# Gate products moved among the last query sums, next key projection at the loop's end, mask begun beside the taps

## The reference, cut to what matters

```
q = silu(conv4(x @ Wq.T));  k = silu(conv4(x @ Wk.T));  v = silu(conv4(x @ Wv.T))
q = q * rsqrt(sum(q*q) + 1e-6);  k = k * rsqrt(sum(k*k) + 1e-6)      # per head
delta = delta_rule(q, k, v, beta)                                    # chunked, T = (I + tril(kb k'))^-1
paths = (fir3(v), fir63(v), delta, v)
gate_in = concat([x] + [mean and var per head of each path])         # 256 + 32 columns
hmid = gelu(gate_in @ gate_w1.T + gate_b1)                           # 512 wide
probs = softmax((hmid @ gate_w2.T + base_bias) / temp)               # 4 paths per head
x1 = layernorm(x + rmsnorm(sum(probs * paths)) @ Wo.T)
```

## Time and profile before

| | us |
|---|---|
| median of 3 runs | 1892.97 (1891.18 to 1901.68) |
| the profiled execution | 1894.72 |
| its span | 1893.0 |
| PE busy (matmul) | 1496.2 (79%) |
| DVE busy | 1315.3 (69%) |
| ACT busy | 950.1 (50%) |
| POOL busy | 440.7 (23%) |

### The profile page before, as it was taken

How to read it: one execution, slowest core, us unless ns; L and a number is a source line. 1 busy time by engine, 2 the same in 40 slices (tenths; PEclk the granted TensorE clock), 3 DMA queues, 4 the chain that set the end, 5 groups by cost and what they waited for, 6 DMA issues and landing times. The chain is left out here.

```text
span 1893.0 us, 40332 instructions
## 1 busy us (share of the span) xinstructions
PE 1496.2 (79%) x12507; PEld 1108.8 (59%) x12508; DVE 1315.3 (69%) x3331; ACT 950.1 (50%) x1998; POOL 440.7 (23%) x473
## 2 busy tenths in 40 slices
PE   6775165979999999999999999887436999999800
PEld 3445134747747747657557567476225888888700
DVE  6995155677787887887887887875455555554488
ACT  6772061356555644654655555542443555555434
POOL 6884200000030040040030210300223333333300
PEclk9997585989999999999999999998758999999955
DMA  5558642023243243333333333232524533333295
GB/s 197 190 163 256 154 101 58 3 67 94 71 127 92 62 122 102 78 91 101 87 89 106 95 106 90 79 97 76 196 91 140 192 105 101 104 104 101 77 385 190
DMA packets 297370, 224.34 MB, mean 119 GB/s; under 512 B 173472, under 2 KB 265632, under 8 KB 296960
## 3 DMA queue, kind: packets, MB, share of 16 engines
q1 hardware_dynamic: 225600, 158.84, 29.0%
q0 software_dynamic: 15232, 43.53, 6.4%
q10 hardware_dynamic: 56384, 19.93, 4.1%
HBM read 130.42 MB, written 91.82 MB: 117 GB/s over the span
## 5 line engine op out<-in xcount | busy, mean ns | idle before, releaser
L1462 DVE SCALAR_TENSOR_TENSOR B_conv<-B_ps_x,B_cw,B_conv 128x511 f32<-128x511 f32 (+2 forms) x192 | 143.5, 748 | 65.9 <-ACT B_conv L1176 59.3
L2031 POOL DMA_INDIRECT y_d<-C_yb,C_dest x136 | 132.1, 971 | 232.0 <-ACT C_yb L2142 229.7
L422 POOL DMA_INDIRECT xs_d<-x,slot_u x128 | 133.4, 1042 | 137.4 <-DVE m_acc L1857 100.6
L688 POOL MEMSET B_z<- 128x256 f32 (+4 forms) x40 | 5.5, 191 | 674.6 <-DMA B_z<-scr_a 674.6
L1176 ACT ACTIVATE B_conv<-B_ps_x,B_cw 128x512 f32<-128x512 f32 x64 | 43.7, 683 | 167.6 <-PE B_ps_x L745 167.3
L2261 DVE TENSOR_TENSOR C_av<-C_sg,C_ps_g 128x256 f32<-128x256 f32 x136 | 57.3, 421 | 94.6 <-ACT C_sg L2136 94.6
L2065 PE MATMUL C_ps_g<-C_w_high,C_xt_high 128*128 x272 | 119.5, 439 | 0.4 <-issue 0.4
L745 PE MATMUL B_ps_x<-B_xa,B_wk 128*128 128x512 f32 x128 | 67.5, 655 | 63.8 <-DVE B_sel L1454 44.9
L2273 DVE TENSOR_TENSOR C_avt_low<-C_ps_a,C_avt_high 128x256 fp32r<-128x256 f32 x136 | 57.7, 425 | 83.5 <-ACT C_avt_high L2131 83.5
L2065 PE MATMUL C_ps_g<-C_w_high,C_xt_low 128*128 x272 | 107.7, 396 | 0.0
L2065 PE MATMUL C_ps_g<-C_w_low,C_xt_high 128*128 x272 | 107.0, 393 | 0.0
(11 more groups left out here) (330 smaller groups left out, 4250.6 us busy)
## 6 DMA issues: line engine op xcount, KB each, us to landing
C_xb<-xs_d SPq DMA_DIRECT2D x136, 132.0 KB, 2.1
C_w_high<-y_d SPq DMA_DIRECT2D x12, 1024.0 KB, 14.1
A_band<-fir_long POOLq DMA_DIRECT2D x32, 256.0 KB, 5.9
A_work<-xT SPq DMA_DIRECT2D x16, 512.0 KB, 5.0
v_d<-A_v_tok SPq DMA_DIRECT2D x16, 512.0 KB, 3.5
short_d<-A_sh_tok SPq DMA_DIRECT2D x16, 512.0 KB, 3.2
B_xa<-xT SPq DMA_DIRECT2D x8, 1024.0 KB, 5.8
B_v_tok<-v_d SPq DMA_DIRECT2D x8, 1024.0 KB, 5.5
```

What stands on the lines that cost most here:

```text
L422: pool.indirect_dma_start(t["xs_d"][:, :], bass.IndirectOffsetOnAxis(ap=slot_u[:, c:c + 1], axis=0), x1[:, b, j, :], None).then_inc(done, 16)
L1462: V.scalar_tensor_tensor(conv[:, g % 2, k:], X[g % 2][:, :SEQ - k], cw[:, g // 4, gg % CH, 3 - k:4 - k], conv[:, g % 2, k:], ALU.mult, ALU ...
L2031: pool.indirect_dma_start(t["y_d"][:, :], bass.IndirectOffsetOnAxis(ap=dest[:, q:q + 1], axis=0), yb[:, u], None).then_inc(y_out[u], 16)
```

## The change

- **Gate on four banks.** The hidden chunks get four banks, `hidden = (X[0], X[1], B3, B4)`, and PE's gate splits into `from_x` (the two products with x of one chunk) and `from_stats` (the product with the statistics). The four `from_x` of the first half move out of the gate into `stage1b`, among the last query sums: one after the sum of group 5, three after that of group 6. The spins that stood there (two after each of the groups 5 to 7 and three after `rank`) go, and two take their place behind group 7. The last step, which prepares no pair, runs them inside its gate.
- **First key projection.** `project(i + 2, 0)` moves from the start of the next step to the end of this one, behind the second product; its wait for `x_out` goes. The spins at that place go from four to two, and the last two steps have none.
- **Mask.** It no longer waits for `mt_in[1]`; instead it waits for the count of `mixd` that DVE's first `weigh` gives.

```diff
+        hidden = (X[0], X[1], B3, B4)
...
                 def mask_at(p):
 
                     pool.wait_ge(at_kept, 8 * (p + 1))
-                    pool.wait_ge(mt_in[1], 32 * (p + 1))
+                    need(pool, mixd, 4 * (p - 1) + 1)
...
+                def from_x(i, b, c):
+                    pe.wait_ge(xg_in[b], 16 * (i + 1))
+                    for k in range(CH):
+                        mm(hidden[c][:], w1x[:, k, c * P:(c + 1) * P], xg[b][:, k, :], start=k == 0, stop=False)
+
+                def from_stats(c):
+                    mm(hidden[c][:], w1s[:, c * P:(c + 1) * P], st_t[:], start=False, stop=True).then_inc(gate_mm, 1)
...
-                    for g in range(5, 8):
-                        select(p, g)
-                        if last is not None:
-                            if g == 5:
-                                pe.wait_ge(a_kept[1], 4 * (p + 1))
-                            spin(B3, 2)
+                    if first:
+                        for g in range(5, 8):
+                            select(p, g)
+                    else:
+                        select(p, 5)
+                        for k in a_kept:
+                            pe.wait_ge(k, 4 * (p + 1))
+                        from_x(p - 1, 0, 2)
+                        select(p, 6)
+                        from_x(p - 1, 0, 3)
+                        pe.wait_ge(taps, 24 * p + 21)
+                        from_x(p - 1, 0, 0)
+                        pe.wait_ge(taps, 24 * (p + 1))
+                        from_x(p - 1, 0, 1)
+                        select(p, 7)
+                        spin(B5, 2)
                     turn_norms(p, 1)
                     if last is not None:
                         rank(last)
-                        spin(B3, 3)
...
+                def gate(i, has_prev, has_next):
+
+                    if has_prev:
+                        pe.wait_ge(rt, RT * (i - 1) + 1)
+                    pe.wait_ge(st_dve, ST * (i + 1))
+                    turn_stats(i, 0)
+                    if not has_next:
+                        pe.wait_ge(taps, 24 * (i + 1))
+                        for c in range(HID_CH):
+                            from_x(i, 0, c)
+                    pe.wait_ge(st_kept, 2 * i + 1)
+                    for c in range(HID_CH):
+                        from_stats(c)
+                    turn_stats(i, 1)
+                    for c in range(2):
+                        pe.wait_ge(gelu_ok, 8 * i + c + 1)
+                        from_x(i, 1, c)
...
+                    logits(i, 0)
+                    pe.wait_ge(st_kept, 2 * i + 2)
+                    for c in range(2):
+                        from_stats(c)
+                    for c in range(2, HID_CH):
+                        from_x(i, 1, c)
+                        from_stats(c)
+                    pe.wait_ge(raw_kept, 2 * i + 1)
+                    logits(i, 1)
...
-                    if has_next:
-                        hold(pe, x_out, 16 * (i + 1))
-                        project(i + 1, 0)
                     merges(i, has_prev, has_next)
...
                     if has_next:
                         at_rest(i + 1)
-                        spin(X[1], 4)
...
+                    if has_after:
+                        project(i + 2, 0)
+                        spin(X[1], 2)
```

More of the change, by code:

```diff
@@ L996, in recur, with turn_stats @@
                         within(i, s)
[L998 to L1002, removed]
+                def turn_stats(i, b):
                     for j in range(TPB):
@@ L1006, in gate, with logits @@
                     w.then_inc(st_turned, 1)
-                    pe.wait_ge(xg_in[b], 16 * (i + 1))
+                def logits(i, b):
+                    pe.wait_ge(gelu_ok, 8 * i + 4 * (b + 1))
                     for c in range(HID_CH):
[L1009 to L1022, removed]
+                        w = mm(B2[c * LANE:(c + 1) * LANE, :], w2[:, c, :], hid[:, c, :], start=True, stop=True)
+                    w.then_inc(raw_mm, 1)
+                def gate(i, has_prev, has_next):
[14 more added lines that the diff above has]
+                        from_x(i, 1, c)
+                    if has_next:
                         for k in a_kept:
@@ L1026, in gate @@
                         pe.wait_ge(r_ub, 4 * (i + 1))
-                    for c in range(HID_CH):
-                        w = mm(B2[c * LANE:(c + 1) * LANE, :], w2[:, c, :], hid[:, c, :], start=True, stop=True)
-                    w.then_inc(raw_mm, 1)
+                    logits(i, 0)
[7 more added lines that the diff above has]
+                    logits(i, 1)
                 def turn_logits(i, b, has_prev, has_next):
@@ L1112, in _, with step @@
                 select(0, 3)
-                stage1b(0)
+                stage1b(0, first=True)
                 at_first(0)
                 at_rest(0)
-                def step(i, has_prev, has_next):
-                    if has_next:
-                        hold(pe, x_out, 16 * (i + 1))
-                        project(i + 1, 0)
+                project(1, 0)
+                def step(i, has_prev, has_next, has_after):
                     merges(i, has_prev, has_next)
@@ L1133, in step @@
                         rank(i - 1)
-                    for b in range(2):
-                        gate(i, b, has_prev, has_next)
+                    gate(i, has_prev, has_next)
                     if has_next:
@@ L1311, in recur, with gate, keep_stats @@
                             keep_x1(i - 1, 1)
-                def gate(i, b):
-                    half = 2 * i + b
-                    act.wait_ge(st_turned, half + 1)
-                    need(act, gate_mm, 4 * half)
-                    A(st_t[:], TR[0:3 * STATS, :], ACT.Copy).then_inc(st_kept, 1)
-                    need(act, raw_mm, half)
-                    for c in range(HID_CH):
-                        act.wait_ge(gate_mm, 4 * half + c + 1)
-                        A(hid[:, c, :], X[c % 2][:], ACT.Gelu, bias=b1[:, c:c + 1]).then_inc(gelu_ok, 1)
-                    act.wait_ge(raw_mm, half + 1)
-                    A(raw_logits[:, b, :], B2[:], ACT.Copy).then_inc(raw_kept, 1)
+                def gate(i):
+                    def keep_stats(b):
+                        act.wait_ge(st_turned, 2 * i + b + 1)
+                        need(act, gate_mm, 8 * i + 4 * b)
+                        A(st_t[:], TR[0:3 * STATS, :], ACT.Copy).then_inc(st_kept, 1)
+                    keep_stats(0)
+                    for b in range(2):
+                        need(act, raw_mm, 2 * i + b)
+                        for c in range(HID_CH):
+                            act.wait_ge(gate_mm, 8 * i + 4 * b + c + 1)
+                            A(hid[:, c, :], hidden[c][:], ACT.Gelu, bias=b1[:, c:c + 1]).then_inc(gelu_ok, 1)
+                        if b == 0:
+                            keep_stats(1)
+                        act.wait_ge(raw_mm, 2 * i + b + 1)
+                        A(raw_logits[:, b, :], B2[:], ACT.Copy).then_inc(raw_kept, 1)
                 def rms(i, b):
@@ L1410, in step @@
                         keep_routes(i - 1)
-                    for b in range(2):
-                        gate(i, b)
+                    gate(i)
                     A(warm[:], eps5[:], ACT.Exp)
```

11 lines of the change are left out of this document (6 added, 5 removed).

## The result

| | before | after |
|---|---|---|
| median, us | 1893.07 (1891.18 to 1901.68) | 1932.24 (1929.17 to 1936.42) |
| profiled execution | 1894.72 | 1934.13 |
| span | 1893.0 | 1932.4 |
| ratio of the times | | 1.0199, 95% interval 1.0161 to 1.0237 |

Slower, as forecast, but by 39 us instead of 21, and outside the range (1880 to 1926).

What follows compares the result with a forecast made beforehand. What delays the norm on DVE was taken to delay everything, the gate being hidden but for 0.67 us. Six steps of +4 us gave 1919, 1917 as median, less 6 times 0.4: 1914 us; range 1880 to 1926.

Steps and rivals of the forecast that it cites:

- signs that it named for being right: Sums 5.7 us apart, norm waiting 3, no softmax or tap wait, PE idle 4 before merge at clock 0.5, slower merge.
- Term 1: Last query sums on PE: three x product pairs between the sums of groups 6 and 7 delay the norm by 3.2 us.
- Term 2: DVE's holes at logits, exponential and first tap pay back 0.67, 0.6 and 1.45 us; in sum the 3.2 us, no more.
- Term 3: PE before the merge: work ends at 832.8, loads land at 839.1, so PE idles about 6 us (3.5 to 7.5).
- Term 4: Merge on PE begins at the low clock: L897 4.8 us later, about 4 us lost a step (3 to 5.5).
- the first rival, a cured fall: The clock's fall before L936 goes away, a step gains 2.5 of its 4 us: 1902 us; chance 0.22.
- The start of the block … I count as zero: Start of the block, where the projection had warmed the clock: no change in time.
- The first pass: First of the loop's seven passes, without spins among the sums and with a later gate: zero (0 to +3 us).
- the cure of 2.4: Taken off the sum because some steps may lose their clock fall before L936: 6 times 0.4 us.
- The rival of the held clock: Clock stays at 1.00 through the merge, 0.5 to 3 us gained a step: 1871 to 1889 us; chance 0.23.

Runs made afterwards that it cites:

- e3: The changed kernel with the sum of group 7 put ahead of two x products, in place of two spins: 1909.41 us, 1.0077 of the kernel before.
- e9: The changed kernel with PE waiting, after the step's last two spins, for the store of scr_xt to land: 1928.38 us, 1.0170 of the kernel before.
- e13: The changed kernel with ACT's five loads of the solved blocks moved behind the first tap and the weighing of values: 1926.62 us, 1.0140 of before.
- e14: The changed kernel with both e9's wait on PE and e13's later ACT loads: 1924.78 us, 1.0132 of the kernel before.
- e17: The changed kernel with the loop's boundary on PE moved ahead of the second product, order of work unchanged: 1917.33 us, 1.0118 of the kernel before.
- e1: The changed kernel with four spins instead of two at the step's end: 1930.17 us, 1.0180 of the kernel before.
- e8: The kernel before with only the first key projection moved to the loop's end, two spins instead of four: 1898.83 us, 0.9995 of before.
- e15: The changed kernel with e3's order, nine spins with e9's wait among them, and e13's later ACT loads: 1895.03 us, 0.9979 of the kernel before.
- e18: The changed kernel with e3's order, nine spins, e13's later loads, e17's boundary and the first mask back behind its loads: 1905.83 us, 1.0049 of before.

## Why the prediction was wrong

- **Direction and mechanism: right.** The x products delay the norm, DVE's holes pay that back, PE runs dry before the merge, the clock falls. All the signs that it named for being right are in the profile after.
- **Term 1: right**, 3.24 us from sum to sum against 3.2; e3 gave back 3.5 a step.
- **Term 2: right.** The logits' wait went, of 1.13 us 0.38 remain, the tap's wait went, L1759 takes 1.23. DVE then waits 1.68 us for PE.
- **Term 3: the step that failed** is "issued at 832.33 and half a microsecond later, now +3.2, plus 3.1 to land". It took the time from store to loads (2.78 us) and the landing as fixed. The store landed 1.98 us later and the loads came 0.95 us later behind that (4.55 instead of 3.6), in sum 2.9, about what the idle stretch of 8.84 has over the forecast's 6. In its place the runs show PE's code packet on the store (e9: gone when PE waits) and ACT's loads, which the change itself brings ahead of SP's (e13). Together the two are worth 2.0 of the 2.9 us (e14).
- **Term 4: mis-sized the other way.** With the merge at 839.1 and L897 at 845.59 + 4.8 the stretch was forecast as 11.3 us; it is 10.38. From L954 to L987 6.41 us are left of 7.79: the first rival, a cured fall, came in part. Counted from the recurrence ahead, the merge of the step shown starts 2.3 us later than before (forecast 0.3), L899 to L915 adds 3.6 (forecast 4.5), and 0.5 comes back up to L954 (forecast 0.8): 5.4 for 4. So a loss too small in term 3 and one too large in term 4 partly cancel, and the sum is nearer than its terms. Over six steps it is 5.0 each where I had 4 less 0.4: 30 for 22.
- **"The start of the block … I count as zero": wrong**, 4.8 us, of which 3.6 are the first mask on DVE's row. The earlier trace rows held the warning, a row of DVE that ran only when POOL had finished, and I used it for the loop alone.
- The first pass cost 1.8, inside its 0 to 3. The 2.9 us behind the last recurrence I can't place; over all profiles that stretch varies from 626 to 631 us (628.0 before, 631.0 after).
- The sum: 6 times 4 measured 29.9 (+5.9), the cure of 2.4 was taken off on top, and 4.8 + 1.8 + 2.9 stood at zero: 17.8 of the 18.2 us between 1914 and 1932.24. The cure was also reckoned wrongly: a third of 2.5 us is 0.8 and not 0.4, which would have made it 1912. Smaller slips change nothing (5.6 for 5.5 in term 4, 1871 for 1872 and 1925 for 1926 among the rivals). The rival of the held clock did not come; e17 shows that it could have, with the same order of work and another place of the branch.

## What to carry to other kernels

When a step is moved earlier, list what it issues and what its engine fetches, and ask which transfer on the critical path is then in flight: here two neighbours of the store and the loads made the merge 2 to 3 us later in each loop step, and no engine's own row showed them. Where an idle engine is kept busy only for its clock, cover the whole wait or don't count on it: behind waits of 1.5 to 2.4 us the merge still took 3 us longer, behind one of 0.46 us it did not. And check the first and last pass of a pipelined loop by themselves, since a wait dropped there has nothing left to stand on.

## What the runs showed of the hardware that I had not expected

- A single 0.02 MB packet of instructions, 0.9 us on one DMA engine, went with a 512 KB store that landed 1.9 to 2.1 us later (4.7 to 4.9 us instead of 2.8), and with the packet moved the store was back at 2.8 (e9). Where it came is moved by a wait on PE (e9) or by the place of a branch (e17), not by two more spins ahead of it (e1).
- PE waited 1.5 to 1.8 us inside the merge (e8, e15) and 2.9 to 3.4 us behind a loop's branch (e17, e18) for instructions.
- A stall and a fall of the clock upstream can be worth more than they cost: in e17 they filled the idle stretch behind which the clock had fallen in the merge, and in the pass without them (7.30 us idle) it fell there.
